# Causal attention of one stage: fp32 scores of four heads in strips of 32 partitions, instead of three-part bf16 scores of one head after the other

## The chip, the cores and the metric

The kernel runs on one core of a Trainium2 chip. The metric is the device time of one launch in microseconds. TensorE (PE) does the matmuls, VectorE (DVE), ScalarE (ACT) and GpSimd (POOL) the elementwise work, SyncE (SP) issues the transfers.

## The reference, cut to what matters

The model is a chain of some ten stages on an activation x of 4 batches x 1024 positions x 128 channels. The change touches one of them alone, the causal attention with 16 heads of 8 channels, applied to the layernorm of x and added to x:

```python
def _L1_attn_a_ref(x, WQ, WK, WV, WO):
    ...
    mask = jnp.where(jnp.triu(jnp.ones((S, S), dtype=bool), k=1), -jnp.inf, 0.0).astype(x.dtype)
    Q, K, V = (heads(WQ), heads(WK), heads(WV))
    score = jnp.einsum('bhqd,bhkd->bhqk', Q, K) / jnp.sqrt(jnp.asarray(D_K, x.dtype))
    score = score + mask
    score = score - jnp.max(score, axis=-1, keepdims=True)
    score = jnp.exp(score)
    score = score / jnp.sum(score, axis=-1, keepdims=True)
    out = jnp.einsum('bhqk,bhkd->bhqd', score, V)
    out = out.transpose(0, 2, 1, 3).reshape(B, S, E)
    return out @ WO
```

## The kernel before

`causal_attention` (L1010 on) works in 16 rounds, one for each batch and group of four heads. A round has two passes over the scores, each over the lower triangle in blocks of 128 positions. The **first pass** (`ring_step`, product L1305) puts q x k with queries on the partitions into one of three PSUM banks; DVE takes the row maxima (L1450). When all of a round's maxima are there, one product turns them (L1313), and SP writes them into the operand of the **second pass** (`second`, L1328), which computes k x q with keys on the partitions and the maxima subtracted inside the product, into three other banks; ACT takes the exponential (L1417). Its results are multiplied with the values (`values`, L1341): four heads in four column strips of 32, fp32, into the last two banks. A column of ones among the values gives the sums, which go by DMA to be inverted; DVE divides (L1468), and eight products with WO (L1318) and two additions (L1460) put the round's heads into x.

The scores must be as good as fp32 ones, and are computed in bf16: after the projections (L1277), q and k are split into three bf16 parts (ACT L1399 and L1393, DVE L1432, POOL L1227), the parts go to DRAM (`causal_parts`), and `load_round` fetches them with 18 transfers a round, so that 72 rows hold all nine combinations and one product gives the sum. Three further rows hold the three parts of the maxima, which POOL splits (L1235 to L1242) and for which it clears rows (L1261). Each head's product uses the full array. Wherever a block lies on the diagonal, a second full-array product with the identity adds a 128 x 128 mask (L1308, L1330), 32 in each pass of a round.

PE's order is written out: `items` lists a round's 38 second-pass units and its value products, and after each unit as many steps of `ring_steps` are issued as its cost is of the whole. These steps are the first pass of the next round, of which the first 18 units (`LEAD`) come one round earlier still, the turn and the two output steps of the round before. So both passes alternate on PE, each ahead of its own three banks:

```python
pe.wait_ge(s1_free.sem, s1_free.at(n - RING + 1))     # first pass: a bank that DVE has read
pe.wait_ge(probs.sem, probs.at(n - RING + 1))         # second pass: a bank that ACT has read
```

Before the first round's second pass stand its first pass and 18 steps of the next, with nothing of the second pass beside them.

## Time and profile before

| | us |
|---|---|
| median of 3 runs (lowest to highest) | 3485.97 (3484.61 to 3486.74) |
| profiled execution | 3486.21 |
| its span | 3484.3 |
| PE busy over the span | 2833.4 |
| the stage, from the first projection (L1277) to the last addition to x (L1460) | 735.3 to 1366.6 |
| of it, up to the first score (L1305) | 34.3 |

The profile is of one execution. A busy time is the sum of an engine's instructions, where those that overlap count once; a mean is that of one record, from its start to its end, and matmuls overlap, so that a mean is longer than the step from one start to the next. An fp32 product has two records in the trace (the program issues 16 at L1277, the trace has 32), a bf16 product has one. PEclk is the clock granted to TensorE as a share of 2.4 GHz.

### The profile page before, as it was taken

How to read it: one execution, taken by the hardware profiler on the slowest of the kernel's cores; microseconds unless marked ns; L12 is line 12 of the kernel's file. 1: busy time of each engine (PE TensorE's matmuls, PEld its weight loads, DVE VectorE, ACT ScalarE, POOL GpSimd, SP SyncE). 2: the span in 40 equal slices, each digit the busy share in tenths (PEclk: the TensorE clock that was granted, in tenths of full speed). 3: DMA queues.
4: the chain of work that ended last, by engine and by line, in shares of the span. 5: the costliest groups of instructions: out<-in, count | busy, mean ns of one | idle time of the engine just before them, and what ended most of it. 6: DMA issues, size and time to landing. Idle time of an engine off the chain costs nothing. (4 is left out here: it accounts for less than half of the span.)

```text
span 3484.3 us, 62796 instructions
## 1 busy us (share of the span) xinstructions
PE 2833.4 (81%) x22143; PEld 1662.3 (48%) x22143; DVE 2478.2 (71%) x4050; ACT 1756.8 (50%) x3569; POOL 1837.0 (53%) x1184
## 2 busy tenths in 40 slices
PE   3677468568999995999999993677677599999998
PEld 1211257443444442677667752223222277757774
DVE  5599646558777763777577755698599777767774
ACT  3544125134556553677467732544444277737762
POOL 3499211130111101888188822698299598729871
PEclk9699678779999997999999996899899899999999
DMA  3355000042222210112112210343054112211121
GB/s 90 79 162 151 8 7 1 8 116 69 38 44 38 44 24 24 38 40 47 30 36 44 43 25 5 109 158 121 31 169 157 56 40 44 45 24 42 42 45 40
DMA packets 176158, 203.21 MB, mean 58 GB/s; under 512 B 108358, under 2 KB 122396, under 8 KB 175388
## 3 DMA queue, kind: packets, MB, share of 16 engines
q1 hardware_dynamic: 175868, 199.41, 22.2%
q8 instruction: 174, 2.85, 0.4%
q14 instruction: 116, 0.95, 0.1%
HBM read 138.36 MB, written 9.44 MB: 42 GB/s over the span
## 5 line engine op out<-in xcount | busy, mean ns | idle before, releaser
L319 POOL TENSOR_TENSOR arena<-arena 128x1024 f32<-128x1024 f32 x192 | 451.3, 2351 | 61.1 <-DVE arena L336 34.0
L1450 DVE TENSOR_REDUCE causal_peak_parts<-psum 128x1 f32<-128x512 f32 (+3 forms) x608 | 375.9, 658 | 114.9 <-PE psum L1308 69.6
L2047 POOL TENSOR_TENSOR arena<-arena,w_minus_half 128x16 f32<-128x16 f32 x128 | 372.5, 2910 | 97.0 <-DVE arena L1954 97.0
L1417 ACT ACTIVATE arena<-psum 128x512 f32<-128x512 f32 (+1 forms) x608 | 304.0, 597 | 229.5 <-PE psum L1330 106.7
L1889 ACT ACTIVATE arena<-psum,arena 128x128 f32<-128x128 f32 x1024 | 277.8, 382 | 252.8 <-DVE arena L1963 252.8
L336 DVE TENSOR_TENSOR_SCAN arena<-psum,arena 128x1024 f32<-128x1024 f32 x160 | 364.6, 2280 | 27.9 <-POOL arena L319 27.9
L289 ACT ACTIVATE psum<-arena,w_A 128x1024 f32<-128x1024 f32 x192 | 214.5, 1118 | 248.5 <-DVE arena L336 211.4
L2054 POOL TENSOR_TENSOR arena<-arena 128x1024 f32<-128x1024 f32 x124 | 292.4, 2358 | 12.6 <-DVE arena L1948 12.6
L1734 PE MATMUL psum<-w_layer_wqkv,arena 128*128 128x512 f32 x512 | 262.7, 638 | 5.7 <-DVE arena L1948 3.7
L262 PE MATMUL psum<-arena,m_sel 96*128 96x512 bf16 x384 | 117.4, 388 | 180.6 <-DVE arena L351 153.0
L1959 DVE COPY arena<-psum 128x512 f32<-128x512 f32 x128 | 88.5, 691 | 238.0 <-PE psum L1746 238.0
L2059 POOL TENSOR_TENSOR arena<-arena 128x1024 f32<-128x1024 f32 x124 | 236.0, 1903 | 19.1 <-POOL arena L2050 19.1
L277 PE MATMUL psum<-arena,w_ident 128*128 128x512 f32 x512 | 243.4, 598 | 0.0
L1328 PE MATMUL psum<-arena 128*128 128x512 bf16 (+3 forms) x768 | 218.6, 331 | 23.5 <-ACT arena L1417 17.1
L1305 PE MATMUL psum<-arena 128*128 128x512 bf16 (+3 forms) x768 | 214.6, 330 | 21.1 <-DMA arena<-causal_parts 11.6
L262 PEld LDWEIGHTS psum<-arena,m_sel 96*128 (+1 forms) x384 | 23.5, 97 | 342.4 <-issue 174.5
L1954 DVE TENSOR_REDUCE arena<-arena 128x16 f32<-128x1024 f32 x128 | 155.1, 1212 | 31.2 <-ACT arena L1867 31.2
L2187 PE MATMUL psum<-arena,w_layer_w 128*128 128x512 f32 (+1 forms) x384 | 176.4, 595 | 0.0
L1341 PE MATMUL psum<-arena,Z 128*32 128x512 f32 (+3 forms) x1536 | 164.9, 503 | 0.3 <-ACT arena L1417 0.3
L179 POOL TENSOR_TENSOR ln_rstd<-ln_var,w_minus_half 128x8 f32<-128x8 f32 x32 | 53.1, 1659 | 208.9 <-DVE ln_var L108 208.9
L1963 DVE TENSOR_REDUCE arena<-psum 128x8 f32<-128x1024 f32 x128 | 156.6, 1224 | 9.2 <-PE psum L1771 9.0
L1328 PEld LDWEIGHTS psum<-arena 128*128 128x128 bf16 x768 | 72.2, 97 | 180.8 <-issue 81.3
(331 smaller groups left out, 6620.7 us busy)
## 6 DMA issues: line engine op xcount, KB each, us to landing
arena<-scan_rows_large SPq DMA_DIRECT2D x128, 512.0 KB, 3.7
arena<-arena SPq DMA_DIRECT2D x256, 130.0 KB, 2.6
arena<-scan_rows_small SPq DMA_DIRECT2D x128, 256.0 KB, 3.8
arena<-causal_parts SPq DMA_DIRECT2D x288, 64.0 KB
causal_parts<-arena SPq DMA_DIRECT2D x8, 768.0 KB, 9.0
arena<-Z SPq DMA_DIRECT2D x128, 32.0 KB, 1.9
arena<-Z SPq DMA_DIRECT2D x32, 128.0 KB
arena<-in_c_pads SPq DMA_DIRECT2D x4, 896.0 KB
```

The costliest lines, as they stand in the source:

```text
L277: mm = pe.matmul(bank[6 + c][0:M, :], fold, weight[:, s % 2, c * BANK:(c + 1) * BANK], start=False, stop=isinstance(j, int) and j == J - 1 ...
L319: pool.tensor_tensor(inputs[:, s % 2], b_lane[:, s % U], du(*runs[o]), ALU.mult).then_inc(input_up.sem, 1)
L336: dve.tensor_tensor_scan(state[s % U], decay(s), inputs[:, s % 2], 0.0, ALU.mult, ALU.add).then_inc(scanned.sem, 1)
L1305: mm = pe.matmul(o, QK[:, s, 0, col + qt * P:col + (qt + 1) * P], QK[:, s, 1, col + half * BANK:col + half * BANK + size], start=True, sto ...
L1328: mm = pe.matmul(o, QK[:, s, 1, col + kt * P:col + (kt + 1) * P], QK[:, s, 0, col + lo:col + hi], start=True, stop=True)
L1417: act.activation(PT[:, kt % 2, heads[0]:heads[0] + len(heads), lo:hi], place, ACT.Exp, scale=SCALE).then_inc(probs.sem, 1)
L1450: dve.tensor_reduce(part[:, heads[0]:heads[0] + len(heads), qt, half:half + 1].rearrange("p h a -> p (h a)"), place[:, 0:len(heads) * size ...
L1734: mm = pe.matmul(bank[pair_of(i) + m], HT[:, s4, :], w["wqkv"][:, m * INNER:(m + 1) * INNER], start=True, stop=True)
L1889: e = act.activation(PR[:, s, h, :], two(3)[:, h * P:(h + 1) * P], ACT.Exp, bias=LOW[:, s, h:h + 1])
L2047: pool.tensor_tensor(RN[:, s4, :], SS[:, s4, :], k.minus_half[:, 0:2 * HEADS], ALU.pow).then_inc(rn_in.sem, 1)
L2054: pool.tensor_tensor(COS[s4], COS[s4], SIN[s4], ALU.add).then_inc(ready2.sem, 1)
L2059: pool.tensor_tensor(heads, heads, RN[:, s4, :].unsqueeze(2).broadcast_to([P, 2 * HEADS, HD]), ALU.mult).then_inc(rot.sem, 1)
```

## The change

Scores are computed in fp32 from q and k as they are. Head `hh` of a group of four lies in partitions 32 hh to 32 hh + 7, with a row of ones (in k) or of maxima (in q) under it, so each score product reads 8 rows (first pass) or 9 (second) of one strip of 32 rows. A unit is now one head's bank: `first_groups` and `second_groups` list ten groups, each computed for heads 0, 1, 2, 3 (second pass: 2, 3, 0, 1), so both passes have 40 units a round. In six groups of each pass, tiles on the diagonal lie in the bank, and four small bf16 products in the same strip add the mask: the strip's 32 rows select 32 rows of the mask at a time, over 128, 96, 64 and 32 columns (twice that with two diagonal tiles). The parts, their transfers through DRAM, POOL's splitting and clearing go away; q and k are copied by ACT into `QD` and `load_round` makes 8 transfers a round. The value products of a round come in seven visits (`follow`), both halves of a block together. POOL divides; SP packs the quotients of four rounds (`pack`), so that the output product and the additions to x come once in four rounds. Of the 16 projections four stand ahead of the first score, the other 12 between scores. `LEAD` is 20.

```diff
+    QK = k.big[:, 0:2 * GROUP].rearrange("p (s m t) -> p s m t", s=SLOTS, m=2)
+    QD = k.big[:, 2 * GROUP:4 * GROUP].rearrange("p (m t) -> p m t", m=2)
+    PT = k.big[:, 4 * GROUP:6 * GROUP].rearrange("p (s h t) -> p s h t", s=2, h=IN)
...
             for m in range(2):
-                of_round = kept[m].rearrange("b (g e h) a t -> (b g) e h a t", g=GROUPS, h=IN)
-                of_round = of_round[r:r + 1] if isinstance(r, int) else of_round[bass.ds(r, 1)]
-                of_round = of_round.rearrange("r e h a t -> (r e) h a t")
-                for a in range(PARTS):
-                    for c in range(PARTS):
-                        rows = slice((a * PARTS + c) * HD, (a * PARTS + c + 1) * HD)
-                        sp.dma_start(QK[rows, s, m, :].rearrange("e (h t) -> e h t", h=IN), of_round[:, :, a if m else c, :]).then_inc(loaded[s].sem, 16)
-
+                heads = QD[STRIP * g:STRIP * (g + 1), m, b * SEQ:(b + 1) * SEQ]
+                for i in range(IN):
+                    sp.dma_start(QK[STRIP * i:STRIP * i + HD, s, m, :], heads[HD * i:HD * (i + 1)]).then_inc(loaded[s].sem, 16)
 
         CH = [(c, m) for c in range(TOK // BANK) for m in range(2)]
-        CREDITS = ((s1_free, RING), (probs, RING), (pv, 2), (o_in, 1), (zeroed, 1))
+        CREDITS = ((s1_free, RING), (probs, RING), (pv, 2), (o_in, 1))
...
-        first_units = []
-        for qt in range(TPB):
-            for half, (_, n) in enumerate(halves((qt + 1) * P, BANK)):
-                per = BANK // n
-                first_units += [(qt, half, range(h, min(h + per, IN)), n) for h in range(0, IN, per)]
-
-        second_units, after = [], {}
-        for kt in range(TPB):
-            for lo, hi in [(kt * P, BANK), (BANK, SEQ)] if kt * P < BANK else [(kt * P, SEQ)]:
-                per = BANK // (hi - lo)
-                second_units += [(kt, range(h, min(h + per, IN)), lo, hi) for h in range(0, IN, per)]
-            after[kt] = len(second_units)
+
...
+        first_groups = [([(0, 0, [0]), (4, 1, [4])], (0, 2)), ([(1, 0, [0, 1]), (5, 1, [5, 4])], (1, 2)),
+                        ([(2, 0, [0, 1, 2])], (2, 1)), ([(3, 0, [0, 1, 2, 3])], (3, 1)),
+                        ([(4, 0, [0, 1, 2, 3])], None), ([(5, 0, [0, 1, 2, 3])], None), ([(6, 0, [0, 1, 2, 3])], None),
+                        ([(6, 1, [4, 5, 6])], (2, 1)), ([(7, 0, [0, 1, 2, 3])], None), ([(7, 1, [4, 5, 6, 7])], (3, 1))]
+        first_units = [(hh,) + u for u in first_groups for hh in range(IN)]
+
+        second_groups = [([(0, 0, 512)], 0, 0, 1, -4), ([(0, 512, 1024)], 0, 512, 0, 0), ([(1, 128, 512)], 1, 128, 1, 0), ([(1, 512, 1024)], 1, 512, 0, 0),
+                         ([(3, 384, 512), (2, 256, 512)], 0, 128, 2, 1), ([(2, 512, 1024)], 0, 512, 0, 1), ([(3, 512, 1024)], 1, 512, 0, 2),
+                         ([(4, 512, 1024)], 0, 512, 1, 3), ([(5, 640, 1024)], 1, 640, 1, 4), ([(7, 896, 1024), (6, 768, 1024)], 0, 640, 2, 5)]
+        second_units = [(hh,) + u for u in second_groups for hh in (2, 3, 0, 1)]
...
-        LEAD = 18
-        SHORT, LONG = N1 + 1, N1 + 3
+        LEAD = 20
+        SHORT = N1 + 1
         soon = [("soon", i) for i in range(LEAD)]
-
-        def ring_steps(before, more):
-
+        INVERSE_AT, OUT_AT = 13, 30
...
-        INVERSE_AT, DIVIDE_AT, OUT_AT = 11, 20, 27
-
-
-        follow = {min(after[kt] + 2, N2 - 1): kt for kt in range(TPB - 2)} | {1: TPB - 2, 2: TPB - 1}
+            return SHORT + LEAD + sum(len(steps_of(q)) for q in range(r))
+
+        def turn_at(r):
+
+            return ring_start(r - 1) + steps_of(r - 1).index(("turn", 0)) if r else N1
+
+        follow = {10: [0], 18: [1], 26: [2], 30: [3], 35: [4], 39: [5], 3: [6, 7]}
...
+                def pack(r):
+                    sp.wait_ge(divided.sem, divided.at(r + 1))
+                    if r % GROUPS == 0 and r:
+                        sp.wait_ge(s1_up.sem, s1_up.at(ring_start(r + 1) + OUT_AT + 2))
+                    for hh in range(IN):
+                        row = STRIP * (r % GROUPS) + HD * hh
+                        sp.dma_start(OP[row:row + HD, :], ON[STRIP * hh:STRIP * hh + HD, :]).then_inc(packed.sem, 16)
...
-                def split_maxima(r, n, s, count):
-
-                    pool.wait_ge(s1_free.sem, s1_free.at(n + 1))
-                    if count is not None:
-                        pool.wait_ge(*count)
-                    pool.sem_inc(fed.sem, 1)
-                    pool.tensor_copy(lowb[:, 0, :], low[:, 0, :]).then_inc(split.sem, 1)
...
-                        pool.memset(QK[PEAK:PEAK + PARTS, (s + 3) % SLOTS, 0, :], 0.0).then_inc(zeroed.sem, 1)
...
+                def divide(r):
+                    pool.wait_ge(sums_in.sem, sums_in.at(16 * IN * (r + 1)))
+                    pool.wait_ge(packed.sem, packed.at(16 * IN * r))
+                    pool.tensor_tensor(ON, OT, INV, ALU.mult).then_inc(divided.sem, 1)
...
-                        for at, hh in enumerate(heads):
-                            col = hh * SEQ
-                            o = out[:, at * size:(at + 1) * size]
-                            diag = half == (qt * P) // BANK
-                            mm = pe.matmul(o, QK[:, s, 0, col + qt * P:col + (qt + 1) * P], QK[:, s, 1, col + half * BANK:col + half * BANK + size],
-                                           start=True, stop=True)
-                            if diag:
-                                mm = pe.matmul(o[:, size - P:size], k.identb, mask[:, 0, :], start=False, stop=True, skip_group_check=True)
+                        at = 0
+                        for qt, half, keys in tiles:
+                            runs = [keys] if keys == sorted(keys) else [[x] for x in keys]
+                            for run in runs:
+                                size = len(run) * P
+                                mm = pe.matmul(out[:, at:at + size], QK[rows, s, 0, qt * P:(qt + 1) * P], QK[rows, s, 1, run[0] * P:run[0] * P + size],
+                                               start=at == 0, stop=True, skip_group_check=True)
+                                at += size
+                        if diag:
+                            place = out[:, diag[0] * P:(diag[0] + diag[1]) * P].rearrange("p (d t) -> p d t", t=P)
+                            strip = slice(STRIP * hh, STRIP * (hh + 1))
+                            for c in range(4):
+                                mm = pe.matmul(place[:, :, STRIP * c:P], PICK[strip, c, :], MASK[strip, c, 0:diag[1], STRIP * c:P],
+                                               start=False, stop=True, skip_group_check=True)
                         mm.then_inc(s1_up.sem, 1)
...
-                            mm = pe.matmul(out[:, j * P:(j + 1) * P], ON[:, i * BANK + j * P:i * BANK + (j + 1) * P], WS[:, g, :], start=True, stop=True)
+                            mm = pe.matmul(out[:, j * P:(j + 1) * P], OP[:, i * BANK + j * P:i * BANK + (j + 1) * P], WS, start=True, stop=True)
...
-                    for at, hh in enumerate(heads):
-                        col = hh * SEQ
-                        o = bank[RING + n % RING][:, at * size:(at + 1) * size]
-                        mm = pe.matmul(o, QK[:, s, 1, col + kt * P:col + (kt + 1) * P], QK[:, s, 0, col + lo:col + hi], start=True, stop=True)
-                        if lo == kt * P:
-                            mm = pe.matmul(o[:, 0:P], k.identb, mask[:, 1, :], start=False, stop=True, skip_group_check=True)
+                    at = 0
+                    for kt, lo, hi in tiles:
+                        mm = pe.matmul(bank[RING + n % RING][:, at:at + hi - lo], QK[rows, s, 1, kt * P:(kt + 1) * P], QK[rows, s, 0, lo:hi],
+                                       start=at == 0, stop=True, skip_group_check=True)
+                        at += hi - lo
+                    if diag:
+                        place = bank[RING + n % RING][:, 0:diag * P].rearrange("p (d t) -> p d t", t=P)
+                        strip = slice(STRIP * hh, STRIP * (hh + 1))
+                        for c in range(4):
+                            mm = pe.matmul(place[:, :, 0:STRIP * (c + 1)], PICK[strip, c, :], TURNED[strip, c, 0:diag, 0:STRIP * (c + 1)],
+                                           start=False, stop=True, skip_group_check=True)
                     mm.then_inc(s2_up.sem, 1)
...
+                    for half in range(kt // 4, 2):
+                        lo = max(kt * P, half * BANK) - half * BANK
+                        for hh in range(IN):
+                            mm = pe.matmul(bank[6 + half][STRIP * hh:STRIP * (hh + 1), lo:BANK], VS[:, kt, hh, :], probs_place(kt, half, hh),
+                                           start=kt == 0, stop=kt == 4 * half + 3)
+                    mm.then_inc(pv.sem, 1)
...
+    blocks = np.where(n > c4 + strip, MASKED, 0.0)
+    c["c_causal_blocks"] = bf16(np.stack([blocks, blocks], axis=2)).reshape(P, 8 * P)
+    turned = np.where(n < c4 + strip, MASKED, 0.0)
+    c["c_causal_turned_blocks"] = bf16(np.stack([turned, turned], axis=2)).reshape(P, 8 * P)
+    c["c_ones"] = np.ones((4, SEQ), dtype=np.float32)
```

Three places of the order, before and changed. On PE in the middle of a round, both passes on the diagonal; before:

```order
L1328 MATMUL psum<-arena 128x512
L1330 MATMUL psum<-causal_mask,w_identb 128x128
L1305 MATMUL psum<-arena 128x256
L1308 MATMUL psum<-causal_mask,w_identb 128x128
L1305 MATMUL psum<-arena 128x256
L1308 MATMUL psum<-causal_mask,w_identb 128x128
```

and with the change:

```order
L1250 MATMUL psum<-arena 128x512
L1278 MATMUL psum<-arena 128x512
L1285 MATMUL psum<-causal_turned_mask,arena 128x32
L1285 MATMUL psum<-causal_turned_mask,arena 128x64
L1285 MATMUL psum<-causal_turned_mask,arena 128x96
L1285 MATMUL psum<-causal_turned_mask,arena 128x128
L1250 MATMUL psum<-arena 128x512
```

Between the two passes' products stood one mask product a head; now four of them follow a product, and all are in one strip.

On PE at a visit to the values, before (one half of a block):

```order
L1305 MATMUL psum<-arena 128x384
L1308 MATMUL psum<-causal_mask,w_identb 128x128
L1341 MATMUL psum<-arena,Z 32x512 x4
L1305 MATMUL psum<-arena 128x384
L1308 MATMUL psum<-causal_mask,w_identb 128x128
```

and with the change (both halves in one visit):

```order
L1257 MATMUL psum<-arena 128x96
L1257 MATMUL psum<-arena 128x64
L1257 MATMUL psum<-arena 128x32
L1298 MATMUL psum<-arena,Z 32x512 x8
L1278 MATMUL psum<-arena 128x384
L1285 MATMUL psum<-causal_turned_mask,arena 128x32
L1285 MATMUL psum<-causal_turned_mask,arena 128x64
```

The visits are fewer, and the rows around them are strips.

On POOL from one round's maxima to the next, before:

```order
L1235 CAST causal_low_parts<-causal_low 32x128
L1237 TENSOR_TENSOR causal_low<-causal_low,causal_low_parts 32x128
L1240 CAST causal_low_parts<-causal_low 32x128
L1242 TENSOR_TENSOR causal_low_parts<-causal_low,causal_low_parts 32x128
L1249 COPY Z<-arena 128x32x8
L1261 MEMSET arena 3x4096
```

and with the change, from the clearing ahead of the rounds on:

```order
L1194 MEMSET Z 128x1024
L1195 MEMSET causal_peak_parts 128x64
L1201 COPY Z<-arena 128x32x8 x2
L1206 TENSOR_TENSOR Z<-Z 128x1024
L1201 COPY Z<-arena 128x32x8
```

POOL keeps the copy of the values, and has the division that was DVE's.

## Rows read from the trace of the kernel before

**Rows 1.** Page, the engines: busy time, share of the span, instructions.
```profile
PE 2833.4 (81%) x22143; PEld 1662.3 (48%) x22143; DVE 2478.2 (71%) x4050; ACT 1756.8 (50%) x3569; POOL 1837.0 (53%) x1184
```

**Rows 2.** Window of the rounds: PE, PEld, DVE, ACT, POOL busy (count), PEclk, DMA share, GB/s.
```profile
805.00:1310.00 505.00, 484.50 (x3962) 216.38 (x3960) 380.47 (x631) 292.25 (x577) 67.14 (x82) 1.00 0.22 39
```

**Rows 3.** Window of one round, and the copies (L1408) that begin and end it.
```profile
943.15:977.83 34.68, 33.30 (x276) 15.11 (x274) 26.54 (x45) 19.81 (x40) 5.29 (x7) 1.00 0.26 41
...
L1408 ACT COPY Z<-psum x2: 1047/1047/1047, 943.1 to 977.8; 128x1024 f32<-128x1024 f32 x2
```

**Rows 4.** Groups of that round: busy us, mean ns, idle before.
```profile
L1328 PE MATMUL psum<-arena 128*128 128x512 bf16 (+3 forms) x49 | 14.0, 331 | 1.2 <-ACT arena L1417 1.0
L1341 PE MATMUL psum<-arena,Z 128*32 128x512 f32 (+3 forms) x96 | 10.2, 498 | 0.0
L1308 PE MATMUL psum<-causal_mask,w_identb 128*128 128x128 bf16 x32 | 6.1, 219 | 0.0
```

**Rows 5.** Timeline of PE, full clock: start us, us, operation.
```profile
1104.46 0.39 PE L1305 MATMUL psum<-arena 128*128 128x512 bf16 x1
1104.69 0.22 PE L1308 MATMUL psum<-causal_mask,w_identb 128*128 128x128 bf16 x1
1104.75 0.38 PE L1305 MATMUL psum<-arena 128*128 128x512 bf16 x1
1105.11 1.07 PE L1341 MATMUL psum<-arena,Z 128*32 128x512 f32 x8
```

**Rows 6.** Timeline of PE at the projections.
```profile
742.25 1.88 PE L1277 MATMUL psum<-arena 128*128 128x512 f32 x4
```

**Rows 7.** Windows of L2451 alone where its column tile changes: PE, PEld, PEclk.
```profile
439.24:439.35 0.11, 0.11 (x3) 0.11 (x2) 1.00 0.00 0
439.68:439.79 0.11, 0.11 (x7) 0.11 (x3) 1.00 0.00 0
```

**Rows 8.** Windows and groups under 64-row products, 20 us.
```profile
84.00:88.00 4.00, 4.00 (x5) 0.95 (x4) 0.44 (x1) 2.49 (x3) 0.00 (x0) 0.50 0.14 33
100.00:104.00 4.00, 4.00 (x6) 0.86 (x5) 1.22 (x1) 2.70 (x4) 0.00 (x0) 0.50 0.14 33
...
L478 PE MATMUL psum<-arena,w_delta 64*128 64x512 f32 x8 | 7.2, 1057 | 0.0
```

**Rows 9.** Windows and group under other 64-row products.
```profile
361.00:366.00 5.00, 4.33 (x31) 4.36 (x32) 1.56 (x2) 0.00 (x0) 0.00 (x0) 0.81 0.00 2
366.00:370.00 4.00, 4.00 (x20) 4.00 (x20) 1.22 (x1) 0.00 (x0) 0.00 (x0) 0.50 0.00 0
...
L565 PE MATMUL psum<-w_W_down,arena 64*128 64x128 f32 x64 | 11.8, 370 | 1.6 <-PEq L212 1.6
```

**Rows 10.** Windows and group under 128-row products.
```profile
2157.00:2161.00 4.00, 3.98 (x10) 1.47 (x8) 3.93 (x4) 0.71 (x1) 0.00 (x0) 1.00 0.00 0
...
L668 PE MATMUL psum<-Z,w_w_inT 128*128 128x512 f32 x28 | 12.8, 617 | 0.0
```

**Rows 11.** Groups: DVE in the stage, and POOL of the page.
```profile
L1450 DVE TENSOR_REDUCE causal_peak_parts<-psum 128x1 f32<-128x512 f32 (+3 forms) x608 | 375.9, 658 | 114.9 <-PE psum L1308 69.6 <-PE psum L1305 39.5
...
L319 POOL TENSOR_TENSOR arena<-arena 128x1024 f32<-128x1024 f32 x192 | 451.3, 2351 | 61.1 <-DVE arena L336 34.0
```

**Rows 12.** First pass, second pass and projections: first and last start.
```profile
L1305 PE MATMUL psum<-arena x768: 218/379/528, 769.6 to 1311.6; 128*128 128x512 bf16 x96, 128*128 128x128 bf16 x32, 128*128 128x256 bf16 x32, 128*128 128x384 bf16 x32
...
L1328 PE MATMUL psum<-arena x768: 218/378/634, 803.6 to 1347.6; 128*128 128x512 bf16 x96, 128*128 128x384 bf16 x32, 128*128 128x256 bf16 x32, 128*128 128x128 bf16 x32
...
L1277 PE MATMUL psum<-arena x32: 592/592/1061, 735.3 to 756.6; 128*128 128x512 f32 x32
```

**Rows 13.** Timeline of the end.
```profile
1360.76 1.23 DVE L1468 TENSOR_TENSOR Z<-Z 128x1024 f32<-128x1024 f32 x1 [4.94 <-DMA Z<-causal_inverses]
1365.86 0.69 DVE L1460 TENSOR_TENSOR X<-X,psum 128x512 f32<-128x512 f32 x1 [1.02 <-PE psum L1318]
```

**Rows 14.** Maxima: their DMA issues on SP.
```profile
L1180 SPq DMA_DIRECT2D arena<-causal_low_parts x48: 502/591/597, 795.8 to 1317.8; - x48
```

More of the change, by code:

```diff
@@ L1206, in body @@
+                maxima(0)
+                for r in range(ROUNDS):
+                    if r:
+                        invert(r - 1)
+                    if r + 1 < ROUNDS:
+                        maxima(r + 1)
+                    if r and r + 3 < ROUNDS:
+                        sp.wait_ge(qk_in.sem, qk_in.at(4 * ((r + 3) // GROUPS + 1)))
                         sp.wait_ge(s2_up.sem, s2_up.at(r * N2))
-                        load_round(sp, r + 3, (s + 3) % SLOTS)
-                rounds(sp, body)
+                        load_round(sp, r + 3)
+                    if r:
+                        pack(r - 1)
@@ L1331, in second, with values @@
                     mm.then_inc(s2_up.sem, 1)
[L1333 to L1335 removed]
+                def values(kt, r):
                     pe.wait_ge(probs.sem, probs.at(r * N2 + after[kt]))
```

400 lines of the change are left out of this document (159 added, 241 removed).

## The prediction

> **What bounds the kernel now.** The page gives only that PE is the busiest engine [rows 1]. The window of the rounds comes next: from 805 to 1310 us PE is busy for 484.50 of 505.00 us at full clock, DVE for 380, ACT for 292, POOL for 67 [rows 2]. PE binds there, and the others matter through the banks they free. One round, from one copy L1408 to the next, is 34.68 us [rows 3]. Its groups show the work [rows 4]: scores by L1328 and L1305, their masks by L1308 and L1330 (32 each), values by L1341. Their means overlap, so prices come from starts. A bf16 score of 512 columns takes 0.23 us (1104.46 to 1104.69) and its mask 0.06 (1104.69 to 1104.75); the eight records of a value visit, four strips at once, take 1.07 us together [rows 5]. Two fp32 products of 512 columns with the full array (four records) take 1.88 us with the tail [rows 6]; without it I take **0.86 us a product at full clock**, the same as four bf16 ones.
>
> **What the change does to PE's stream.** Every head has 4608 columns in either pass. Bf16 heads one after another: 2 x 4 x 4608 columns at 0.43 ns = 15.7 us. An fp32 product costs four times as much per column, and four heads in four strips at once would bring that back to 15.7. So the scores alone gain nothing even when all strips overlap; the masks (64 x 0.06 = 3.6 us) would fall to about 2. Everything depends on two questions.
>
> *Do the strips overlap?* Column strips do [rows 5]. But at a change of tile in L2451 (sixteen records to a tile, 0.11 us each) the windows show three records touched in a slice of 0.11 us, and seven 0.4 us later [rows 7]: the second tile starts only when the first has its last few left, one running and three waiting, though its operands had long been there. So the queue ahead of a tile is short and in order. A score unit without a diagonal is two records, and the next strip starts beside it. A unit with a diagonal is two fp32 records and four masks (six or more); with three waiting, the next strip starts only when the first one's fp32 records are through. I take it that **units with a diagonal run one after another**, with masks hidden under the next strip's product.
>
> *Does the clock hold?* Under 64-row products PE was busy 4.00 of 4.00 us in five windows from 84 to 104 us (first and last shown) and the granted clock stood at 0.50, that is 1.2 GHz, all that time; a 512-column record took 1057 ns on average [rows 8]. Under another 64-row group it fell from full to 0.50 with PE as busy [rows 9]. Under 128-row products, equally busy, it stood at 1.00, with 617 ns for a record [rows 10]; that is also where the rounds of before stand [rows 2]. The strips read 8 or 9 rows of 32. The nearest rows are the 64-row ones, and the change goes further the same way. I take **1.2 GHz for most of the stage**: 1.71 us for an fp32 product.
>
> **A round after it.** Units with a diagonal have 20480 of the 36864 columns (heads times both passes), 40 products' worth: 40 x 1.71 = 68.4 us. The 32 units without one, at three at a time (three banks each pass), 32 x 1.71 / 3 = 18.2. Values, four heads at once, 4608 columns: 9 x 1.71 = 15.4. Seven value visits switch from strips to columns and back, some 0.3 us each, 2. Output and turn, 1. Waits for banks and at the ends, 5, which is what the 34.7 us round had beyond its stream (15.7 + 3.6 + 9 x 0.86 + 2.2 of output and turn = 29.3). Sum **110 us** against 34.7. Bounds of the round: full overlap at full clock 33 below; above, no overlap even of the plain units, 146.
>
> **The whole.** Against the profiled execution's 3486.21 us (the median of the runs is 3485.97, the same to 0.01%):
> - 15 rounds with both passes: 15 x (110 - 34.7) = +1130.
> - The last round has only the second pass: 34 + 9 + 15 + 6 = 64 instead of about 26: +38.
> - The 60 first-pass units ahead of the first second-pass product, now 33.9 us (769.6 to 803.6) [rows 12]: 24 and 16 units with a diagonal, 33 products' worth, x 1.71 = 57, plus 20 plain ones, 11: 68, +34.
> - Before the first score, 34.3 us (735.3 to 769.6) [rows 12]: no parts, no DRAM. Four projections (about 3 us), a copy (0.7), eight issues at 0.59 [rows 14] and a landing near 2 put it at 747 to 748: -22. Bounds -26 and -10 (SP issues 20 constants first). The twelve other projections, 12 x 0.86 = 10 us at full clock, now run between scores: +5, the rest beside waits.
> - The end: a division on POOL at 2.35 us (by the row of the same shape, [rows 11]) for 1.23 on DVE [rows 13], and four `pack` transfers, 4 x 0.59 and a landing: +5.
>
> Sum +1190, so **about 4676 us**.
>
> Costed at nothing: DVE and ACT (26.5 and 19.8 busy of 34.68 [rows 3]; 40 reductions of at most 0.66 [rows 11] are 26 us of a round of 110), POOL's copies, `load_round`'s 8 issues for 18, the maxima's four for three without POOL's splitting. Their cover is PE's own length. If PE's round fell to 33, DVE's 26 and the bank ring would be late next: a bank costs 0.86 + 0.2 + 0.66 + 0.1 = 1.8 us from start to start, so three banks give 40 units in 24 us, to which the value visits (10) add part of their time. SP has a new wait, `pack`, with the next `invert` and `maxima` behind it; the division it waits for is done in the first half of a round, and the maxima are wanted at its end, so it holds nobody in a long round.
>
> [...]
>
> **The rivals.**
> - *Strict order.* A strip's product also waits for the masks before it: 17 us more at 1.2 GHz, 127 a round. Against it: the overlap of rows 7. Total 4676 + 16 x 17 = 4950. Chance 0.03.
> - *Diagonals in series, clock full.* 34.4 + 9.2 + 7.7 + 2 + 0.6 + 6 = 60 a round: 15 x 25.3 + 12 + 8 - 22 + 5 = +383, 3869. For it: the value products use all 128 rows and fp32 strips keep PE busy throughout. Against it: rows 8 and 9. Chance 0.13.
> - *Strips overlap, clock low.* 72 product times in threes, 41, plus 15.4, 2, 1 and waits of 12: 72 a round, +560 + 25 + 18 - 22 + 5: 4072. For it: rows 7 are another kind of tile (128 rows, 64 columns). Chance 0.13.
> - *Strips overlap, clock full, the ring binds.* About 40 a round, by the ring's 24, the values' 7.7 and their switches, and waits at both: +80 + 8 + 4 - 22 + 5: 3560. Chance 0.13.
> - *Faster.* All four strips run at once because both passes' banks together give six, so that neither ring decides; masks hide in their strips. 15.7 + 2 + 7.7 + 2 + 0.6 + 5 = 33 a round: 15 x -1.7 - 22 + 3 = -45, **3441**. It decides as soon as a diagonal unit's six records don't hold back the next strip and the clock stays full. For it: PE's order puts different strips next to each other, and L1341 shows four at once. Against it: rows 7, 8 and 9. Chance 0.14.
> - *No change within 0.2%* (7 us, about what a measurement of this kernel tells from none), where the saved 22 us meet a round 1.5 us longer: 0.02.
>
> [...]
>
> **How the numbers follow.** The forecast has 0.42: of its two premises I give the series about 0.6, and the low clock most of it where units are in series, since then one strip of four is at work. Its own range is 4300 (clock full for a third of the time after the long value visits) to 4800 (115 a round and no gain at the start). The range of 8 in 10 reaches from the ring's case, 3560 less its bound of 10, to 4800; outside lie strict order, no change and faster, 0.19 in all. Faster by over 0.2%: 0.14. Within: 0.02. Slower: 0.84.
>
> **What would show it.** The granted clock of the stage near 0.5; starts of diagonal products 1.7 us apart at 1.2 GHz (0.86 at full), in different strips, with the masks beside the next one; plain products of neighbouring strips starting within 0.1 us; PE busy nearly all of a round near 110 us; DVE and ACT idle on PE; a first score near 748. I am wrong if the clock stands at 1.00 through the rounds, or if the product after a mask starts beside the fp32 record of the strip before it.

## The result, and the profile after

The changed kernel takes 4869.01 us (median of 4 runs, 4860.63 to 4913.76) against 3486.35 us for the kernel before (4 runs): a ratio of 1.399, with a 95% interval from 1.391 to 1.408. The profiled execution has a span of 4858.8 us, 1374.5 more than before.

The page of the changed kernel: engines, the granted clock in 40 slices, and the two groups of score products (line, operation, count, then busy us, mean ns, and the idle time before):

```profile
PE 4238.6 (87%) x25659; PEld 2317.0 (48%) x25663; DVE 2461.8 (51%) x4026; ACT 1792.6 (37%) x3585; POOL 1791.4 (37%) x1105
...
PEclk7896865555555555555555699999889999999999
...
L1250 PE MATMUL psum<-arena 8*128 8x512 f32 (+3 forms) x1664 | 976.5, 818 | 3.9 <-DMA arena<-arena 3.1
L1278 PE MATMUL psum<-arena 9*128 9x512 f32 (+3 forms) x1536 | 904.2, 839 | 0.7 <-ACT arena L1365 0.7
```

Before, PE was busy 2833.4 us [rows 1]; now it is 1405 us more, and all of the longer time is PE's. From the seventh slice to the twenty-second, all of them in this stage, the clock stands at 5 tenths. The windows of the stage say it more exactly (columns as in [rows 2]):

```profile
745.00:865.00 120.00, 115.11 (x404) 56.43 (x405) 41.41 (x68) 8.31 (x13) 0.40 (x1) 0.54 0.08 15
1000.00:2000.00 1000.00, 1000.00 (x4040) 458.71 (x4036) 214.16 (x358) 186.38 (x340) 21.93 (x16) 0.52 0.03 5
2000.00:2700.00 700.00, 698.32 (x2876) 320.16 (x2873) 135.14 (x226) 141.68 (x259) 18.78 (x13) 0.52 0.03 5
```

PE is busy for 1000.00 of 1000.00 us, at 0.52 of the clock; DVE and ACT are busy 214 and 186 us of 1000, where they were 380 and 292 of 505 [rows 2]. One round, between two copies L1357 (L1408 of before, [rows 3]):

```profile
1121.70:1244.70 123.00, 123.00 (x492) 56.13 (x490) 25.83 (x43) 22.48 (x43) 2.75 (x2) 0.51 0.03 5
...
L1357 ACT COPY Z<-psum x2: 1006/1006/1006, 1121.7 to 1244.7; 128x1024 f32<-128x1024 f32 x2
```

123.0 us for 34.68. Its groups, which answer to [rows 4] (96 records of values in both):

```profile
L1250 PE MATMUL psum<-arena 8*128 8x512 f32 (+3 forms) x105 | 64.0, 829 | 0.0
L1278 PE MATMUL psum<-arena 9*128 9x512 f32 (+3 forms) x97 | 60.2, 857 | 0.0
L1298 PE MATMUL psum<-arena,Z 128*32 128x512 f32 (+3 forms) x96 | 17.0, 848 | 0.0
L1285 PE MATMUL psum<-causal_turned_mask,arena 32*128 32x32 bf16 (+3 forms) x96 | 13.1, 273 | 0.0
```

Now the place where I expected products in series. The timeline of PE after a value visit (start, length, operation; an fp32 product is two records):

```profile
1440.28 2.07 PE L1278 MATMUL psum<-arena 9*128 9x512 f32 x2
1442.15 0.23 PE L1285 MATMUL psum<-causal_turned_mask,arena 32*128 32x32 bf16 x1
1442.15 1.00 PE L1250 MATMUL psum<-arena 8*128 8x384 f32 x1
1442.22 0.40 PE L1285 MATMUL psum<-causal_turned_mask,arena 32*128 32x64 bf16 x3
1442.95 0.84 PE L1250 MATMUL psum<-arena 8*128 8x384 f32 x1
1443.60 0.31 PE L1257 MATMUL psum<-arena 32*128 32x128 bf16 x1
1443.60 1.00 PE L1278 MATMUL psum<-arena 9*128 9x384 f32 x1
```

The second-pass product of one strip (L1278, 512 columns) starts at 1440.28. The first-pass product of another strip and another bank (L1250) comes at 1442.15, in the very moment in which the first of the four masks (L1285) starts; the three other masks, which stand ahead of it in the program, start after it. The next strip's L1278 comes at 1443.60, again with the first mask of the strip before it. It wasn't waiting for a bank: DVE's last reduction before it had ended at 1438.66 and ACT's last exponential at 1435.80.

```profile
1438.10 0.56 DVE L1392 TENSOR_REDUCE causal_peak_parts<-psum 128x1 f32<-128x384 f32 x1 [0.89 <-PE psum L1257]
...
1435.20 0.60 ACT L1365 ACTIVATE arena<-psum 128x512 f32<-128x512 f32 x1 [3.01 <-PE psum L1285]
```

The weight loads there:

```profile
1440.28 0.50 PEld L1278 LDWEIGHTS psum<-arena 9*128 9x128 f32 x2 [1.66 <-issue]
1441.30 0.15 PEld L1285 LDWEIGHTS psum<-causal_turned_mask,arena 32*128 32x128 bf16 x1 [0.52 <-issue]
1442.15 0.15 PEld L1285 LDWEIGHTS psum<-causal_turned_mask,arena 32*128 32x128 bf16 x1 [0.71 <-issue]
1442.15 0.28 PEld L1250 LDWEIGHTS psum<-arena 8*128 8x128 f32 x1
```

The load for the mask is made at 1441.30, behind the second record, ahead of its product. The load of L1250's weights starts only at 1442.15, with the product itself.

The first and last starts of projections and of both passes (rows of before: [rows 12]), and the end of the stage ([rows 13]):

```profile
L1220 PE MATMUL psum<-arena,w_WK x16: 592/1061/1222, 740.5 to 812.9; 128*128 128x512 f32 x16
...
L1250 PE MATMUL psum<-arena x1664: 267/907/1218, 753.9 to 2633.7; 8*128 8x512 f32 x86, 8*128 8x128 f32 x57, 8*128 8x384 f32 x28, 8*128 8x256 f32 x14
...
L1278 PE MATMUL psum<-arena x1536: 270/842/1218, 864.0 to 2717.4; 9*128 9x512 f32 x104, 9*128 9x128 f32 x60, 9*128 9x384 f32 x28
```

```profile
2741.89 0.69 DVE L1401 TENSOR_TENSOR X<-X,psum 128x512 f32<-128x512 f32 x1 [1.02 <-PE psum L1268]
```

The first score comes at 753.9 us (before: 769.6), but the first second-pass product at 864.0 (803.6).

### The profile page after: what moved, and what is told of

It is laid out like the page before. It is cut to its first block and busy times, and to the rows that moved or that the text cites. A ratio compares the mean times of both kernels' runs of the same rounds, so it can differ in the third digit from the quotient of the medians.

```text
span 4858.8 us, 69583 instructions
## 1 busy us (share of the span) xinstructions
PE 4238.6 (87%) x25659; PEld 2317.0 (48%) x25663; DVE 2461.8 (51%) x4026; ACT 1792.6 (37%) x3585; POOL 1791.4 (37%) x1105
## 5 line engine op out<-in xcount | busy, mean ns | idle before, releaser
L1392 DVE TENSOR_REDUCE causal_peak_parts<-psum 128x1 f32<-128x512 f32 (+3 forms) x640 | 401.7, 636 | 1420.0 <-PE psum L1257 839.3
L1250 PE MATMUL psum<-arena 8*128 8x512 f32 (+3 forms) x1664 | 976.5, 818 | 3.9 <-DMA arena<-arena 3.1
L1365 ACT ACTIVATE arena<-psum 128x512 f32<-128x512 f32 (+1 forms) x640 | 346.5, 555 | 1544.8 <-PE psum L1285 1209.3
L1278 PE MATMUL psum<-arena 9*128 9x512 f32 (+3 forms) x1536 | 904.2, 839 | 0.7 <-ACT arena L1365 0.7
L1278 PEld LDWEIGHTS psum<-arena 9*128 9x128 f32 x1536 | 348.7, 299 | 303.7 <-issue 256.2
L1250 PEld LDWEIGHTS psum<-arena 8*128 8x128 f32 x1664 | 372.7, 299 | 72.0 <-issue 45.1
L1257 PEld LDWEIGHTS psum<-arena 32*128 32x128 bf16 x1536 | 189.7, 140 | 265.2 <-issue 254.1
L1285 PEld LDWEIGHTS psum<-causal_turned_mask,arena 32*128 32x128 bf16 x1536 | 148.8, 130 | 295.0 <-issue 280.9
L1298 PE MATMUL psum<-arena,Z 128*32 128x512 f32 (+3 forms) x1536 | 268.9, 841 | 0.0
L1285 PE MATMUL psum<-causal_turned_mask,arena 32*128 32x128 bf16 (+5 forms) x1536 | 208.6, 272 | 0.0
```

Of the source, the lines that this page charges most:

```text
L1250: mm = pe.matmul(out[:, at:at + size], QK[rows, s, 0, qt * P:(qt + 1) * P], QK[rows, s, 1, run[0] * P:run[0] * P + size], start=at == 0, s ...
L1278: mm = pe.matmul(bank[RING + n % RING][:, at:at + hi - lo], QK[rows, s, 1, kt * P:(kt + 1) * P], QK[rows, s, 0, lo:hi], start=at == 0, sto ...
L1285: mm = pe.matmul(place[:, :, 0:STRIP * (c + 1)], PICK[strip, c, :], TURNED[strip, c, 0:diag, 0:STRIP * (c + 1)], start=False, stop=True, s ...
L1298: mm = pe.matmul(bank[6 + half][STRIP * hh:STRIP * (hh + 1), lo:BANK], VS[:, kt, hh, :], probs_place(kt, half, hh), start=kt == 0, stop=kt ...
L1365: act.activation(PT[:, slot, hh, at:at + size], bank[RING + n % RING][:, 0:size], ACT.Exp, scale=SCALE).then_inc(probs.sem, 1)
L1392: dve.tensor_reduce(spot, place[:, 0:len(tiles) * size].rearrange("p (h t) -> p h t", t=size), AX_X, ALU.max).then_inc(s1_free.sem, 1)
```

## The experiments

**Theories.** A: what waits ahead of a strip is a short queue in program order, and four masks fill it. C: the clock falls because few rows are read. The first four runs try each alone. E1 to E11 are one run each, and the kernel before took 3480.66 to 3497.51 us beside them; the changed kernel's own four runs lie 53 us apart, so smaller differences than that are read from the traces alone.

**E1, no masks.** `for c in range(4)` over the mask products of both passes becomes `range(0)`.

```diff
-                            for c in range(4):
+                            for c in range(0):
```

> The changed kernel without its mask products: the diagonal is not masked in either pass, all else stays. Theory A (a short queue in program order: the next strip's product starts only when at most three records of the strip before are waiting behind the running one, and four masks are what holds it back): every unit is now two to six fp32 records, strips overlap three or four at a time, a round falls from 122 us to 70 to 80 at 1.2 GHz, the time to 4050 to 4250 us; lower still if the clock rises with it. Theory B (strips don't overlap in this kernel for another reason, and the masks are work like any other): at most the 20480 bf16 columns of masks go, 17 us at 1.2 GHz, and as they run beside the next product nearly nothing is won: 4600 to 4860 us.

4065.44 us, in theory A's range; a round is 68.2 us between most copies, just under the 70 to 80 that it gave. The window:

```profile
1100.00:1600.00 500.00, 498.70 (x2149) 229.12 (x2150) 183.47 (x309) 153.09 (x291) 19.25 (x14) 0.54 0.05 9
```

The clock hardly rose (0.54), so most of the 54 us a round is the overlap: the masks' own 20480 columns would be 17 us even in series. It also shows that few rows hold the clock low when the strips do overlap.

**E2, two masks.** The same with `range(2)`.

> Two of the four mask products of each unit with a diagonal are left out (the upper half of the mask is missing in either pass). Theory A: two fp32 records and two masks are one running and three waiting, so the next strip starts beside the first record: as without masks, 4050 to 4300 us. Theory B1 (a product of another strip waits until the masks before it have begun, however few they are): strips stay in series, a round above 110 us and 4750 to 4860 us.

4237.23 us, 79 to 85 us a round. After a value visit, as in the changed kernel's timeline above:

```profile
1305.51 1.22 PE L1278 MATMUL psum<-arena 9*128 9x512 f32 x1
1305.52 1.00 PE L1250 MATMUL psum<-arena 8*128 8x384 f32 x1
1305.54 1.00 PE L1278 MATMUL psum<-arena 9*128 9x384 f32 x1
```

Three strips start within 0.03 us, each with a unit that has a diagonal. **E3, three masks** (`range(3)`).

> One of the four mask products of each unit with a diagonal is left out. Theory A: the next strip starts when the first one's second fp32 record starts, one record (0.85 us at 1.2 GHz for 512 columns) earlier than with four, so a strip's turn takes about 1.0 us instead of 1.87 and a round 85 to 95 us: 4350 to 4500 us, between the runs with two and with four. Theory B1: 4750 to 4860 us, as with four.

4520.90 us, 95 to 103 us a round; I had 4350 to 4500 and 85 to 95, so both came out above the range; the order of the three runs is as expected. The timeline at such a visit:

```profile
1313.59 2.07 PE L1278 MATMUL psum<-arena 9*128 9x512 f32 x2
1314.61 1.64 PE L1250 MATMUL psum<-arena 8*128 8x384 f32 x2
1315.42 1.00 PE L1278 MATMUL psum<-arena 9*128 9x384 f32 x1
```

The next strip's product comes at 1314.61, 1.02 us after 1313.59: with the second record of the strip before. So with two masks the next strip starts with the first record, with three with the second, with four when both are through and the first mask starts. Each time three records of the strip before are still waiting behind the running one. That is theory A to the record, and B and B1 are out (whether it is the records or their weight loads that are counted, these runs don't tell, as each record has one load).

**E4, the kernel before with 8 rows.** Only the rows that the score products read are changed.

```diff
-mm = pe.matmul(o, QK[:, s, 0, col + qt * P:col + (qt + 1) * P], QK[:, s, 1, col + half * BANK:col + half * BANK + size],
+mm = pe.matmul(o, QK[0:8, s, 0, col + qt * P:col + (qt + 1) * P], QK[0:8, s, 1, col + half * BANK:col + half * BANK + size],
...
-mm = pe.matmul(o, QK[:, s, 1, col + kt * P:col + (kt + 1) * P], QK[:, s, 0, col + lo:col + hi], start=True, stop=True)
+mm = pe.matmul(o, QK[0:8, s, 1, col + kt * P:col + (kt + 1) * P], QK[0:8, s, 0, col + lo:col + hi], start=True, stop=True)
```

> The kernel before, with its score products reading rows 0 to 7 alone instead of all 128 (only the product of the highest parts is left, and the maxima aren't subtracted, so the values differ); same columns, same number of products, full-array masks and values as they were. Theory C (the clock falls because the score products read few rows): the granted clock of the rounds falls to about 0.5 to 0.7, a round from 34.7 to 50 to 65 us, the time to 3750 to 3950 us. Rival D (the clock falls because the strips, or fp32 in them, leave the array idle otherwise, the number of rows read is nothing): 1.00 as before, 3486 us.

4077.26 us, a round of 73.5, above the 3750 to 3950 us and 50 to 65 that I had written: the masks and values with 128 rows don't lift the clock at all.

```profile
805.00:1310.00 505.00, 505.00 (x1863) 144.17 (x1862) 195.83 (x312) 151.00 (x267) 33.15 (x40) 0.50 0.10 21
```

The same instructions in the same order, PE busy for all of 505 us, and 0.50 instead of 1.00. D is out. Nor is it how busy PE is, by the profile's busy time: PE was busy throughout, at half the clock.

**E5, masks later.** All the work of the changed kernel, in another order on PE: the masks of a unit are put off.

```diff
+                            def masks():
+                                for c in range(4):
+                                    mm = pe.matmul(place[:, :, STRIP * c:P], PICK[strip, c, :], MASK[strip, c, 0:diag[1], STRIP * c:P],
+                                                   start=False, stop=True, skip_group_check=True)
+                                mm.then_inc(s1_up.sem, 1)
+                            pending.append((1, masks))
+                            flush(3)
```

(The second pass likewise; `flush(n)` issues the oldest until n are left, and is called with 0 ahead of plain units, turns, outputs and values.)

> The changed kernel with all its work, but the four masks of a unit are issued after the score products of up to three later units (at most two units of a pass are left without their masks at a time; all masks are issued before a plain unit, a turn, an output or a value visit). Theory A: the score products of neighbouring strips are no longer behind four masks, they run two to three at a time; a round falls from 122 us to 80 to 95 at 1.2 GHz, the time to 4200 to 4450 us. Theory B (the masks' own work, not their place, costs the time): 4800 to 4870 us.

4417.74 us, 90 to 94 us a round: no work is taken out, and 450 us go by the place of the masks in the queue. The clock is as before:

```profile
1100.00:1600.00 500.00, 492.05 (x2680) 233.38 (x2681) 135.84 (x233) 118.76 (x221) 13.68 (x10) 0.54 0.04 7
```

**E6, 32 rows.** Rows 9 to 31 of each strip are cleared once, and the score products read `STRIP * hh` to `STRIP * (hh + 1)`; four more transfers a round clear the row of the maxima.

```diff
-                        rows = slice(STRIP * hh, STRIP * hh + HD)
+                        rows = slice(STRIP * hh, STRIP * (hh + 1))
...
-                    rows = slice(STRIP * hh, STRIP * hh + HD + 1)
+                    rows = slice(STRIP * hh, STRIP * (hh + 1))
```

> The changed kernel with the score products reading all 32 rows of their strip, rows 9 to 31 being zero (a clearing of about 7 us at the start, and 4 more small transfers a round that clear the maxima's row). Theory C1 (the rows that a product reads decide the clock, but one strip of 32 rows at a time is still a quarter of the array): granted clock near 0.5 to 0.6, 4700 to 4890 us. Rival C2 (8 or 9 rows were the trouble and 32 are enough): clock 1.00, a round near 62 us, 3900 us.

4729.00 us, as theory C1 had it: the clock rises from 0.52 to 0.57 only, and the rounds take 103 to 119 us. C2 is out.

```profile
1100.00:1600.00 500.00, 500.00 (x2177) 228.94 (x2176) 116.88 (x194) 100.46 (x184) 13.68 (x10) 0.57 0.03 6
```

**E7, both.** 

> Both edits together: masks later, and 32 rows read of each strip. Theory C1: with two or three strips of 32 rows at work at once the array is used about as in the kernel before; the granted clock rises well above 0.6 (0.8 to 1.00), a round 43 to 60 us: 3650 to 3950 us. Rival C3 (the clock looks at one product's rows, however many run at once): as the run with the masks later alone, within 100 us.

4142.65 us, missed by 190 us: the clock comes to 0.75, not above 0.8, and most rounds take 60.1 us, at a granted clock of 0.89, or 83.2, at 0.61, as the stretches at full clock fall.

```profile
1100.00:1600.00 500.00, 486.41 (x3478) 238.77 (x3478) 177.06 (x306) 152.59 (x289) 19.24 (x14) 0.75 0.05 9
```

But C3 is out: against E5 the round falls by 9 to 32 us with the rows alone.

**E8, the kernel before with 64 rows** (`QK[0:64, ...]` in E4's places). 

> The kernel before with its score products reading rows 0 to 63 of 128 (eight of nine combinations, no maxima; columns and order unchanged). Theory C1: between 128 rows (clock 1.00) and 8 rows (0.50, a round of 73.5 us). Half the rows in 60 per cent of the stream, all rows in masks and values: the clock holds at 0.9 to 1.00, 3486 to 3560 us. If only full-row products hold it: 0.5 to 0.6, above 3900 us.

4046.94 us, most rounds 73.9 us and three between 66 and 68, at a granted clock of 0.58: a clear miss of my own theory's number. 64 rows fare little better than 8.

```profile
805.00:1310.00 505.00, 505.00 (x1900) 149.09 (x1899) 197.73 (x314) 153.34 (x272) 33.16 (x40) 0.52 0.11 21
```

So a mean over all products isn't what I can reckon with; what the runs show is 1.00 with 128 rows in the scores, 0.50 to 0.52 with 64 and with 8, although masks and values were full in all three.

**E9, one strip.** No masks, and every head reads strip 0.

```diff
-                        rows = slice(STRIP * hh, STRIP * hh + HD)
+                        rows = slice(0, HD)
...
-                    rows = slice(STRIP * hh, STRIP * hh + HD + 1)
+                    rows = slice(0, HD + 1)
```

> The changed kernel without masks and with every head reading the rows of strip 0 (so all heads give head 0's scores), to price a product of one strip after another of the same strip. Theory E (the 0.16 us that the changed kernel's trace shows between a diagonal product's first start and the end of its columns is the weight load that can't be done ahead when the strip changes): in one strip the loads go behind the product before, starts of the two 512-column records are 0.85 us apart throughout, a round is 72 x 1.71 + 15.4 + 5 = 143 us, the time about 5200 us (5100 to 5300). Rival (every fp32 product of few rows costs it): 1.87 us a product, a round of 155, 5350 to 5450 us.

5133.27 us, 136 to 144 us a round (I had 143). Three records of 512 columns:

```profile
1499.08 2.76 PE L1278 MATMUL psum<-arena 9*128 9x512 f32 x3
```

(2.76 - 1.06) / 2 = 0.85 us from start to start, against 2.07 - 1.06 = 1.01 at 1440.28 in the changed kernel. The rival is out: the 0.16 us isn't fp32's price. It isn't the masks' either, since this run has none and shows it where a product follows the turn (L1263), which reads all 128 rows:

```profile
1495.50 2.07 PE L1278 MATMUL psum<-arena 9*128 9x512 f32 x2
```

That is 1.01 us again. So it comes where a product starts in another part of the array than the one before it. That it is the weight load fits the load's start, with the product, in the rows of the changed kernel; no run takes the load away. Against E1 the strips' overlap is worth 1068 us.

**E10, projections first.** `for i in range(4): project(i)` becomes `range(len(CH))`, and none is left between scores.

> The changed kernel with all sixteen projections ahead of the first score, none between scores. If the twelve between the scores cost what they show (1.71 us each at 1.2 GHz and a switch to the full array and back), the stretch from first score to first second-pass product falls from 110 us by about 22 to 88, while the first score comes at most 10 us later: 4845 to 4860 us, with the gain seen in the trace. Rival: the stretch is long by the rings (three banks for one pass alone), and stays above 105 us.

4849.72 us, no further from the changed kernel's runs than these are from each other; the gain is seen in the trace:

```profile
L1250 PE MATMUL psum<-arena x1664: 267/938/1219, 760.5 to 2612.3; 8*128 8x512 f32 x86, 8*128 8x128 f32 x57, 8*128 8x384 f32 x28, 8*128 8x256 f32 x14
...
L1278 PE MATMUL psum<-arena x1536: 269/843/1219, 839.7 to 2702.3; 9*128 9x512 f32 x104, 9*128 9x128 f32 x60, 9*128 9x384 f32 x28
```

From first score to first second-pass product 79.2 us instead of 110.1: 31 us for twelve projections, where I had expected 22 here, and 5 in the prediction. The rings don't hold that stretch. 24 us of it reach the rounds' start, 864.0 to 839.7, since the first score comes 7 us later.

**E11, no masks and 32 rows** (E1's and E6's edits). 

> No masks, and 32 rows of each strip read: the strips as free to overlap as this order lets them, with the whole strip's rows at work. Theory C1 (rows at work at once, over all strips, decide the clock): 0.9 to 1.00, a round 38 to 46 us: 3550 to 3680 us; against 4065 us without masks and with 8 or 9 rows. Rival C3: clock 0.54 and 4065 us again.

3709.04 us, 42 to 49 us a round; 29 us above my range, with the clock as expected:

```profile
1100.00:1500.00 400.00, 394.25 (x2646) 186.08 (x2646) 222.92 (x376) 184.39 (x358) 22.37 (x17) 0.94 0.08 13
```

With all strips free and 32 rows in each, the clock is nearly full, with the same idle rows and no more sums to compute. The rounds at a granted clock of 1.00 take 42.0 us. It is the best that this layout did, with the masks left out, and it is still 220 us behind the kernel before.

**E12, the kernel before with one part of the change:** the quotients of four rounds packed, the output product once in four rounds.

```diff
+                def pack(r):
+                    sp.wait_ge(divided.sem, divided.at(r + 1))
+                    if r % GROUPS == 0 and r:
+                        sp.wait_ge(s1_up.sem, s1_up.at(ring_start(r + 1) + OUT_AT + 2))
+                    for hh in range(IN):
+                        row = STRIP * (r % GROUPS) + HD * hh
+                        sp.dma_start(OP[row:row + HD, :], ON[STRIP * hh:STRIP * hh + HD, :]).then_inc(packed.sem, 16)
...
-                            mm = pe.matmul(out[:, j * P:(j + 1) * P], ON[:, i * BANK + j * P:i * BANK + (j + 1) * P], WS[:, g, :], start=True, stop=True)
+                            mm = pe.matmul(out[:, j * P:(j + 1) * P], OP[:, i * BANK + j * P:i * BANK + (j + 1) * P], WS, start=True, stop=True)
```

> The kernel before with one part of the change alone: the quotients of four rounds are packed into 128 rows by SP, so that the eight output products and two additions to x come once in four rounds. The sixteen fp32 records of 128 columns take 16 x 0.107 = 1.7 us of PE a round, and PE binds, so 12 of 16 rounds lose them: 3486 - 12 x 1.7 to 2.2 = 3460 to 3466 us. Rival (they stand in waits that stay): no change, 3480 to 3488 us.

3476.93 us (9 runs) against 3485.94 (14 runs): a ratio of 0.9971, 95% interval 0.9961 to 0.9982. It beats both kernels, the one before by 0.3%; that is 9 us, less than half of the 20 to 26 that I expected. PE's groups from 900 to 1010 us, here and in the kernel before:

```profile
L1339 PE MATMUL psum<-arena 128*128 128x512 bf16 (+3 forms) x152 | 42.7, 329 | 3.4 <-ACT arena L1428 2.6
L1316 PE MATMUL psum<-arena 128*128 128x512 bf16 (+3 forms) x155 | 42.5, 325 | 3.4 <-DVE causal_peak_parts L1461 3.1
L1329 PE MATMUL psum<-arena 128*128 128x128 f32 x16 | 2.2, 282 | 0.0
```

```profile
L1328 PE MATMUL psum<-arena 128*128 128x512 bf16 (+3 forms) x155 | 43.3, 326 | 3.5 <-ACT arena L1417 3.0
L1305 PE MATMUL psum<-arena 128*128 128x512 bf16 (+3 forms) x156 | 42.5, 327 | 0.7 <-DVE causal_peak_parts L1450 0.7
L1318 PE MATMUL psum<-arena,Z 128*128 128x128 f32 x48 | 6.7, 282 | 0.0
```

The output product's busy time falls from 6.7 to 2.2 us, but the first pass's idle time before its products grows from 0.7 to 3.4, by waits for DVE's banks: a good part of what PE gains there it waits for the rings.

## Why the prediction was right or wrong

The direction was right, and so were both mechanisms; the time lay above the range (4869 against 4676, range to 4800). By its own steps, with the stage's times in the traces:

- *Do the strips overlap?* Right, to the record: E1, E2, E3 and E5. The count itself, one running and three waiting, stands in the trace of the kernel before as well, at the change of tile of [rows 7]:

```profile
436.80:439.35 2.55, 2.49 (x12) 2.49 (x13) 0.53 0.00 0
439.34:439.35 0.01, 0.01 (x2) 0.01 (x1) 1.00 0.00 0
439.35:439.37 0.02, 0.02 (x4) 0.02 (x3) 1.00 0.00 0
439.34:439.80 0.46, 0.46 (x10) 0.46 (x9) 1.00 0.00 0
```

Twelve of the first tile's sixteen records of L2451 have started by 439.35, and two of them are in flight. In the next 0.02 us two more start, and by 439.80 eight, where one tile at 0.11 us has four: the thirteenth of the first tile starts together with the first of the second, and three are still to come.

- *Does the clock hold?* Right for the changed kernel: 0.52. My reading that the rows read decide was borne out by E4, E6 with E7, and E11. E4 does it better than the row that I had named: in the window in which the clock fell under the second 64-row group, PE was busy 4.33 of 5.00 us and not throughout, as I had it [rows 9]. The idle 0.67 us are all ahead of 362; from there on PE was busy throughout, 2.00 of 2.00 us at a granted clock of 1.00 and, after the fall, 1.80 of 1.80 at 0.50:

```profile
361.00:362.00 1.00, 0.33 (x3) 0.36 (x4) 0.34 (x1) 0.00 (x0) 0.00 (x0) 1.00 0.00 0
362.00:364.00 2.00, 2.00 (x21) 2.00 (x20) 0.27 (x1) 0.00 (x0) 0.00 (x0) 1.00 0.01 4
364.20:366.00 1.80, 1.80 (x11) 1.80 (x10) 0.75 (x1) 0.00 (x0) 0.00 (x0) 0.50 0.00 0
```

The 1.2 GHz of the prediction and the expectations is this granted clock of 0.50. As an estimate from steps: an fp32 product of 512 columns is priced like four bf16 ones, so like 2048 columns, and takes 0.86 us at 1.00 [rows 6] and 2 x 0.85 at 0.50 (E9, whose windows have 0.50 from 1498.20 to 1501.80), which is 2.4 and 1.2 columns a nanosecond.

That the series of strips keeps the clock low, by which I had raised its chance, isn't needed: E1 has 0.54 with the strips free. The numbers that I drew from it for mixtures (E7, E8) were too high each time.

- *A round*: 110 us predicted, 123.0 measured. The values are as priced: by adding up the columns of that round at the granted clock, 15.5 us (15.4). The score columns cover some 93 us where I had 68.4 + 18.2 = 86.6. One strip alone is at work for 77 of them, and two to four strips for the rest: the plain units ran two at a time on average, not three. What is left without a score or value column is some 14 us where I had 8 (visits, output, waits). **The step that failed is the term 40 x 1.71 = 68.4 us, the price of a product in a unit with a diagonal, taken from products that follow each other in the same rows.** Where a product starts in another strip, its weight load starts with it and not ahead of it (load and product both at 1442.15), and it takes longer: 1.87 us for 512 columns (1150.41 to 1152.28, below), 1.45 for 384 (1442.15 to 1443.60) where 1.28 was reckoned. 48 units x 0.16 = 7.8 us a round. The term of the plain units, 32 x 1.71 / 3 = 18.2, was too small as well, by some 6 us.

```profile
1150.41 1.22 PE L1250 MATMUL psum<-arena 8*128 8x512 f32 x1
...
1152.28 1.22 PE L1250 MATMUL psum<-arena 8*128 8x512 f32 x1
```

- *The rounds together*, from first second-pass product to last copy: 547.2 before, 1857.3 after, +1310 where I had +1168. This is 142 of the 184 us missing. Some luck is in it: 15 rounds that are each 13 us over would be 195, but the last two spacings between copies, 83.4 and 55.0 us where I had 110 and 64, took 36 us back.
- *Ahead of the second pass*: 110.1 instead of 33.9 us, +76 where I had +34 and 5 for projections. E10 shows 31 us for the twelve projections. I had priced them at full clock and mostly hidden, beside a stage that I took to be at half: an error of mine, not of the trace. The other 79 us are the units, for which I had 68. Together 37 us of the missing 184.
- *Before the first score*: -15.7 instead of -22, in its bounds; the 20 small transfers stand ahead on SP.
- *The end*: +5.5 from last copy to last addition, +5 predicted. DVE, ACT, POOL and SP costed at nothing: right but for ACT. In the round of 123.00 us PE is busy throughout; its weight loads wait 5.7 us for ACT and never for the others.
- *The range*: its upper end was 115 us a round. I had named 146 as the bound for units with no overlap, and then gave the range 5 us of the 36 above the forecast; half of them would have held the time.

Against the rivals: the clock-full one is out by the windows, the faster one by E11, which had everything that it asks for but the masks and came to 42 us a round even at full clock, not 33. Two other rivals are nearly met once the masks are left out: *strips overlap, clock low* had 72 a round and 4072 us, E1 has 68.2 and 4065; *the ring binds* had about 40 a round, E11 has 42.0 at full clock. So it was their premise that failed, that the masks don't hold the strips back. Taken alone from the changed kernel, the series is worth 450 us by order alone (E5) and 800 with the masks gone (E1); the clock, once the series is gone, another 356 (E1 to E11).

The rival of strict order, which I had given 0.03, is wrong here: L1250 at 1442.15 starts ahead of three masks that precede it in the program and start from 1442.22 on.

## What to carry to other kernels

Before packing small products into strips, count the records that each strip gets in a row: here what was beyond four of them (one running, three waiting) kept the other strips out (the next strip started 0.01 us after the first with two masks, 1.02 with three, 1.87 with four), so small companion products, masks above all, belong behind the next strips' products (92 us a round instead of 123 for the same work). And read the granted clock under products of as few rows as the new ones will have: a layout that uses a fraction of the rows can halve the clock of everything around it, full-array work included (E4: 0.50 for 505 us, and a value visit of eight records with 128 rows took 1.94 us at 1011.45, where it took 1.07 [rows 5]); idle rows that are zero brought it back only where the strips also overlapped (0.57 in E6, 0.75 in E7, 0.94 in E11). Price a product by a row in which the engine does what it will do then: here the start in another strip added 0.16 us that no row of same-strip products showed.

## What the runs showed of the hardware that I had not expected

- 64 rows of 128 cost nearly as much as 8: most rounds take 73.9 and 73.5 us, the clock at 0.50 to 0.52, with PE busy 505.00 of 505.00 us and masks and values of 128 rows in between.
- Rows that hold only zeros count: with 32 rows instead of 8 or 9, 23 of them zero, the clock went from 0.54 (E1) to 0.94 (E11), and a round from 68 to between 42 and 49 us.
- Four strips of 8 or 9 rows at once run each as fast as one alone: in E1 four products start between 1309.01 and 1309.03, and that of L1250 with 512 columns has its second record at 1310.04, 1.01 us later, as in the changed kernel where it runs alone.
- In the changed kernel the clock came up once or twice in a round, for a short stretch each time, and fell again (1.00 from 1158.19 to 1161.60 and from 1281.07 to 1284.48, 0.50 between): the granted clock of the whole round is 0.51 to 0.53.
- At a granted clock of 0.50, a product of 8 rows and 512 columns that starts in another strip than the one before it took 1.87 us (1150.41 to 1152.28), 0.16 more than the 1.71 of one that follows in the same rows.
